# Second keys' attention scores: copied by ScalarE and masked by GpSimd in place of VectorE's masked multiply, in a newly ordered kernel

## The reference

```
x = x + tanh(g_xattn) * performer(layernorm(x), ctx, ctx)
x = x + tanh(g_ffn)   * ffn(layernorm(x))

performer:  q' = exp(proj_q) + 1e-4,  k' = exp(h_k + proj_k - max h_k) + 1e-4
            out[t] = sum_{s<=t} (q'[t].k'[s]) v[s] / sum_{s<=t} (q'[t].k'[s])
ffn:        h = rms(x); q = h Wq; k,v = (h Wdown) Wup
            att = softmax over heads of q.k;  x = x + (att v) Wo
            h2 = rms(x);  x + sum_e gate_e(h2) * (h2 We[e])
```

## Time and profile before

| | |
|---|---|
| median of 3 runs | 1069.57 us |
| the profiled execution's own time | 1069.42 us |
| span of its core | 1067.6 us, 32201 instructions |
| PE | 1012.6 us busy (95%), 12870 matmuls |
| DVE | 961.4 us busy (90%) |
| ACT | 758.7 us busy (71%) |
| POOL | 752.5 us busy (70%) |
| granted TensorE clock | 0.997 of full speed on average |
| chain that ended last | PE 87%, DVE 5%, POOL 4% |

### The profile page before, as it was taken

One profiled execution on the slowest core, in us unless ns is written; L12 is line 12 of the kernel. 1 busy time (PEld: TensorE's weight loads), 2 busy tenths in 40 slices (PEclk: granted clock), 3 DMA queues, 4 the chain that ended last, 5 costly groups with the idle time before them and its releaser, 6 DMA issues.

```text
span 1067.6 us, 32201 instructions
## 1 busy us (share of the span) xinstructions
PE 1012.6 (95%) x12870; PEld 831.4 (78%) x12870; DVE 961.4 (90%) x2176; ACT 758.7 (71%) x1564; POOL 752.5 (70%) x1111
## 2 busy tenths in 40 slices
PE   1568999999999999999999999999999999999998
PEld 0447788788888888888888888888888888888787
DVE  7778888999999999999999999999999999998996
ACT  6678877776677777668777666877766687776541
POOL 4578877787677778767778766777876677787531
PEclk9989999999999999999999999999999999999999
DMA  9501000011000001100100100010111000000000
GB/s 311 169 21 31 12 24 29 31 31 31 23 28 25 22 31 31 32 21 24 29 22 32 32 31 22 21 32 21 32 32 31 22 22 31 22 21 12 12 11 30
DMA packets 38915, 38.67 MB, mean 36 GB/s; under 512 B 3440, under 2 KB 38512, under 8 KB 38768
## 3 DMA queue, kind: packets, MB, share of 16 engines
q1 hardware_dynamic: 38384, 36.59, 10.9%
q0 software_dynamic: 384, 0.04, 0.0%
HBM read 28.23 MB, written 8.39 MB: 34 GB/s over the span
## 4 chain that ended last, share of the span: by engine, by line
PE 87%; DVE 5%; POOL 4%; issue 1%; ACT 1%; DMA 0%; SPq 0%; POOLq 0%; DVEq 0%; ACTq 0%
PE ps L2302 15%; PE ps L2304 14%; PE ps L2303 14%; PE ps L2333 10%; PE ps L2348 9%; PE ps L2341 5%; PE ps L2317 5%; PE ps L2382 3%; PE ps L2373 3%; PE ps L2296 2%; PE ps L2358 2%; DVE hk L1770 2%; PE ps L2366 1%; PE ps L2367 1%; PE ps L2325 1%
## 5 line engine op out<-in xcount | busy, mean ns | idle before, releaser
L1434 DVE SCALAR_TENSOR_TENSOR z<-ps,gate,z 128x256 f32<-128x256 f32 x512 | 238.5, 472 | 37.9 <-PE ps L2304 29.0
L2302 PE MATMUL ps<-we_hi,h_hi 128*128 128x512 f32 (+2 forms) x640 | 240.5, 376 | 0.6 <-DVE z L1434 0.4
L2304 PE MATMUL ps<-we_hi,h_lo 128*128 128x512 f32 (+2 forms) x640 | 224.1, 350 | 0.0
L2303 PE MATMUL ps<-we_lo,h_hi 128*128 128x512 f32 (+2 forms) x640 | 223.7, 349 | 0.0
L2302 PEld LDWEIGHTS ps<-we_hi,h_hi 128*128 128x128 f32 x640 | 120.4, 188 | 36.7 <-issue 12.6
L2333 PE MATMUL ps<-qf,kf 64*128 64x256 f32 x1024 | 129.2, 391 | 9.1 <-POOL kf L549 4.5
L2304 PEld LDWEIGHTS ps<-we_hi,h_lo 128*128 128x128 f32 x640 | 120.2, 188 | 17.1
L2303 PEld LDWEIGHTS ps<-we_lo,h_hi 128*128 128x128 f32 x640 | 120.8, 189 | 11.5
L2333 PEld LDWEIGHTS ps<-qf,kf 64*128 64x128 f32 x1024 | 96.4, 191 | 29.8 <-issue 11.3
L2348 PE MATMUL ps<-att,v 128*32 128x256 f32 (+1 forms) x2048 | 109.0, 329 | 3.1 <-POOL att L540 0.9
L911 ACT ACTIVATE att<-ps 128x512 f32<-128x512 f32 x32 | 19.1, 597 | 116.8 <-PE ps L2333 116.7
(11 more groups left out here) (232 smaller groups left out, 3079.7 us busy)
## 6 DMA issues: line engine op xcount, KB each, us to landing
x_in<-in_x SPq DMA_DIRECT2D x32, 256.0 KB, 2.6
c_in<-in_ctx SPq DMA_DIRECT2D x32, 256.0 KB, 2.6
out<-z SPq DMA_DIRECT2D x32, 256.0 KB, 2.2
c_chunk<-in_ctx SPq DMA_DIRECT2D x14, 512.0 KB, 8.0
stage<-in_L_ffn_We SPq DMA_DIRECT2D x2, 1024.0 KB, 10.0
c_chunk<-in_ctx SPq DMA_DIRECT2D x2, 256.0 KB, 6.5
stage_b<-in_L_ffn_bup SPq DMA_DIRECT2D x1, 256.0 KB, 6.9
stage_q<-in_L_ffn_Wq SPq DMA_DIRECT2D x1, 256.0 KB, 6.4
```

The lines of the kernel that those rows point to most:

```text
L1434: return dve.scalar_tensor_tensor(out=z[b % 2][:, t, :], in0=ps[:, bank, offset:offset + D], scalar=gate[:, t, ex:ex + 1], in1=z[b % 2][:, ...
L2302: pe.matmul(out, a_hi(c), b_hi(c), start=(c == 0), stop=False)
L2303: pe.matmul(out, a_hi(c), b_lo(c), start=False, stop=False)
L2304: last = pe.matmul(out, a_lo(c), b_hi(c), start=False, stop=(c == C - 1))
```

## The change

The four steps `y00` to `y11` move from VectorE to ScalarE. There they are plain copies, without the mask:

```diff
-                dve.wait_ge(*at("Y0", b))
-                dve.tensor_tensor(att[:, 0, :, 2 * P:3 * P], ps[:, BANK["y00"], :].rearrange("p (j l) -> p j l", j=4),
-                                  causal[:, :].unsqueeze(1).to_broadcast([P, 4, P]), ALU.mult).then_inc(*up("y00", b))
+                act.wait_ge(*at("Y0", b))
+                act.activation(att[:, 0, :, 2 * P:3 * P], ps[:, BANK["y00"], :].rearrange("p (j l) -> p j l", j=4), ACT.Copy).then_inc(*up("y00", b))
...
-                pool.affine_select(out=att[:, 0, :, 0:P], in_=att[:, 0, :, 0:P], compare_op=ALU.is_ge, fill=0.0, base=0,
-                                   pattern=[[0, 4], [1, P]], channel_multiplier=-1).then_inc(*up("m00", b))
+                for own in (slice(0, P), slice(2 * P, 3 * P)):
+                    last = pool.affine_select(out=att[:, 0, :, own], in_=att[:, 0, :, own], compare_op=ALU.is_ge, fill=0.0, base=0,
+                                              pattern=[[0, 4], [1, P]], channel_multiplier=-1)
+                last.then_inc(*up("m00", b))
```

All orders, banks and semaphores are new. The steps `dn`, `qq`, `kv0`, `kv1` now stand in the slot for batch `n` (before, all but `qq` for `n - 1`), the loop runs from 5 to 29 (before, 6 to 30), 25 slots in both. Banks and waits that matter:

```diff
-BANK = dict(stab=0, fk0=6, fk1=4, fk2=3, fk3=7, fq0=0, fq1=2, fq2=4, fq3=1, x000=3, x001=1, x010=0, x011=5,
-            y00=3, y01=7, av0=3, x100=0, x101=2, x110=5, x111=4, y10=1, y11=6, av1=2, nd0=2, nd1=0, ht=1,
...
+BANK = dict(stab=2, fk0=5, fk1=2, fk2=4, fk3=3, fq0=5, fq1=2, fq2=3, fq3=7, x000=0, x001=6, x010=0, x011=1,
+            y00=4, y01=5, av0=3, x100=2, x101=0, x110=1, x111=5, y10=6, y11=2, av1=7, nd0=6, nd1=4, ht=3,
...
             def X10_(b):
+                if b >= 2:
+                    pe.wait_ge(*at("y11", b))
...
             def fkp_(b):
+                if b >= 1:
+                    pe.wait_ge(*at("y11", b - 1))
...
             def fq_(b):
-                if b in (1, 2):
-                    pe.wait_ge(*at("o_x", b - 1))
...
+                if b >= 2:
+                    pe.wait_ge(*at("d_lo", b - 2))
```

More of the change, by code:

```diff
@@ L194, in build @@
             signal("once_pe0", "first_turned first_all most_turned stab_all"),
[L195 to L207, removed]
+            signal("pe0", "fkp fk fq X00 Y1"),
+            signal("pe1", "Y0 av0 av1 av3 nt_t"),
+            signal("pe2", "X01 X11"),
+            signal("pe3", "X10"),
+            signal("pe4", "hn_t dn kv1 s"),
+            signal("pe5", "qq"),
+            signal("pe6", "kv0 pv"),
+            signal("pe7", "o_tr o h2_t1"),
+            signal("pe8", "h2_t0 mm0g mm00"),
+            signal("pe9", "mm1g mm01 mm02"),
+            signal("pe10", "mm10 mm11"),
+            signal("pe11", "mm12"),
+            signal("pe12", "mm13"),
+            signal("pe13", "mm03"),
+            signal("once_dve0", "zero_v1 sel_tok first_least first_most first less_first least_ least stabilizer kept less wq_lo wup_lo"),
             signal("keys_dve0", "key_sums"),
@@ L231, in build @@
[L231 to L241, removed]
@@ new lines, in build @@
+            signal("act4", "ek0 eq1 x000 x001 y10 x101"),
+            signal("act5", "ek3 eq0 y00 y11"),
+            signal("act6", "eq3 x010 nt0 nt1"),
+            signal("act7", "x011 x110 x111"),
+            signal("act8", "y01 x100"),
+            signal("act9", "hn ht_hi d_hi q_bd"),
+            signal("act10", "y p_bd ot_hi"),
+            signal("act11", "k_bd"),
+            signal("act12", "sq h2n h2_hi0 gexp"),
+            signal("act13", "h2_hi1"),
+            signal("once_pool0", "one_tri ident f_scale f_hi f_lo"),
@@ L387, in _ @@
             store_(1)
-            load_x_(7)
-            load_c_(8)
-            for n in range(6, NB + -1):
+            for n in range(5, NB + -2):
                 slot(n)
@@ new lines, in h2n_, with y10_ @@
+            @per_batch
+            def h2n_(b):
+                act.wait_ge(*at("r2", b))
+                for t in range(T):
+                    last = act.activation(h2n[:, t, :], y2[:, t, :], ACT.Copy, scale=r2[:, t:t + 1])
+                last.then_inc(*up("h2n", b))
+            @per_batch
+            def y10_(b):
+                if b == 1:
+                    act.wait_ge(*at("Y1", b))
+                act.wait_ge(*at("av0", b))
+                act.activation(att[:, 0, :, 2 * P:3 * P], ps[:, BANK["y10"], :].rearrange("p (j l) -> p j l", j=4), ACT.Copy).then_inc(*up("y10", b))
@@ L1055, in square_ @@
+                last.then_inc(*up("y", b))
             def square_(b):
```

3002 lines of the change are left out of this document (1497 added, 1505 removed).

## The result

The changed kernel takes 1085.24 us (median of 4, 1082.6 to 1085.54) against 1069.61 (1068.63 to 1070.08) for the kernel before on the same chip: a ratio of 1.0142, 95% interval 1.013 to 1.0154. It is slower by 15.6 us. The forecast was +5.4 us with a range up to 1083, so the direction was right and the size was not.

A forecast was written before the change was run, and what follows sets the result against it. The prediction took PE, busy for 95% of the span, to bound the kernel. 1069.42 us + 2.5 (spacing) + 3.0 (fill) + 0 (tail, new waits) made 1074.9, about 1075 with the 0.15 to the median; range 1066 to 1083.

The forecast's parts named there:

- Term 1: Spacing of PE's matmuls in the loop: the new slot is 0.1 us longer, +2.5 us over 25 slots, bounds 0 and +7.5.
- Term 2: The fill, PE's waits in the early batches: chains to features and scores change, sum +3.0 us, bounds -3 and +9.
- The wait before the scores of batch 3: In the fill: only four product rows stand between fq and the scores, so PE idles 3.7 us: +3.7.
- The gain at fq: In the fill: fq of batch 1 no longer waits 1.98 us for o_x, whose banks it needed: -2.0 us.
- Four copies more, 2.4 us: In the fill, batch 1 to 2: four more copies come before fkp and av3 can go: +2.4 us.
- -1.1: In the fill: 0.95 us before the scores of batch 2 and like pieces, counted as replaced by the new waits.
- 17 to 18 us of idle time: Sign for the fill's sum: PE idle that long between the first scores and 134 us.
- Term 3: Tail and start: the same chains and cover as before, 0 us; bound 2 us either way in the tail.
- the new waits: In the loop, X10 for y11 and fq for ek3 and d_lo: both fit, 0 us, bound +7.5.
- A: Rival: faster, DVE's shorter list gives back 5 us of PE's idle time in the fill, 1064.5 us; chance 0.20.
- B: Rival: one of the loop's two tight places misses, a wait of 0.3 us every slot, 7.5 more, 1082.5; chance 0.20.
- C: Rival: no change, fq's gain and DVE's shorter list cancel the chain, slot as long as before, 1070 us; chance 0.15.

The follow-up runs named there:

- h6: The changed kernel with 40, 24 and 32 matmuls that nothing reads ahead of X01(1), X00(2) and Y0(3), where TensorE idled: 1080.85 us.
- h5: The kernel before with 18 matmuls that nothing reads ahead of fq(1) and 40 ahead of X00(1), where TensorE idled: 1069.37 us.
- n2: The changed kernel with score copies cut to one column, second selects left out, and 40, 24 and 32 unread matmuls in three idle times: 1075.80 us.
- n1: The changed kernel with the moved work left out from batch 1 on: copies of one column, one select per mask: 1082.68 us.
- s1: The changed kernel with pv moved ahead of mm03 in the slot, which adds two changes of the array's division: 1103.4 us.
- b1: The kernel before with fk moved directly behind fkp, which takes away one change of the array's division per slot: 1067.2 us.
- n3: The changed kernel with only the second selects left out, copies kept, and 40, 24 and 32 unread matmuls in three idle times: 1078.57 us.

## Why the prediction was wrong in size

**Sum.** By the two traces, 15.7 us arise so. Up to X00 of batch 7 it is 10.6, with 12 matmuls left undone, which are 2.8 us (12 x 0.23): 13.4 for the same work. Of these, idle time is 8.0 (22.7 against 14.7) and half clock 4.6 (6.4 against 1.8 lost, an estimate). The 0.8 that are left fit five more changes of the array's division in the new fill, counted in the code, which would be some 1 us (not shown by a run). The loop adds 2.8 up to X00 of batch 31 (977.62 before, 991.09 now), less than its two waits alone, and the tail 2.2, which is those 12 matmuls less 0.6.

The experiments price two causes of this: the clock 4.4 (h6 against the changed kernel; 4.1 if the 0.3 that the kernel before gains in h5 is taken off) and the moved work 5.0 (h6 against n2), of which 1.5 is X10's wait in the slots. What is left of the idle time, some 5 us by n1's 19.9 against 14.8, belongs to the new order of the fill: that is read from the waits, and no run that moved steps of the fill gained anything. The parts are differences of separate kernels and overlap, as the clock falls behind idle time.

**Term 1, spacing +2.5: the size came out by luck.** The slot grew by 0.12 us and the time by 3.0, but two waits of 0.12 and 0.07 us, which had no term, are in it: 0.19 of a growth of 0.12. The -0.07 that is left is the spacing together with waits of the same kind that the kernel before has at places of its own (its weight loads wait in each slot, named as for POOL's `att`, for DVE's `h_lo` and for ACT's `att`), and the rows don't part these. So +2.5 us for the spacing is not shown. That a change costs some 0.2 us was right: s1 priced it at 0.17, b1 at 0.20 where it happens and 0.09 on the whole slot.

**Term 2, the fill +3.0: the step that failed.** For the same work it was 13.4 by X00 of batch 7, and 8.8 without the half clock, three times the +3.0 and just inside the bound of +9. The wait before the scores of batch 3 held (3.93 for +3.7). The gain at fq was 1.0 and not 2.0. "Four copies more, 2.4 us" as the whole price of the moved work was too small. It went by ACT's copies alone and gave POOL's second selects no term; n3 gives 2.3 us for the selects and 2.8 for the copies, the slots' share included. The "-1.1" for pieces replaced had no ground: batch 2 got 3.15 where 0.95 was, and 1.89 before dn(0). Its text said that 17 to 18 us of idle time would prove the sum; it is 22.1.

**The clock: missing.** The prediction counted idle microseconds at their own length. Two of its own rows showed 0.93 and 0.92 on either side of a 4.14 us wait; asked of the new waits, they would have warned that half clock comes with such a wait. It had no term and was worth 4.4 us.

**Term 3 and the new waits.** Their 0 failed, though not by much each. The layout had y11 end 0.2 us before X10 is due and d_lo with about as much before fq; X10 waits 0.07 us and fq 0.12, in every slot, together 25 x 0.19 = 4.7 us, within the bound of 7.5. The tail was bounded by 2 us; from X00 of batch 31 to the last matmul it grew from 86.0 to 88.8, with 2.8 us more of PE's busy time left at that point (86.65 and 83.89 us): the work that the new order of the fill had not done yet.

**Rivals.** A is out: DVE's 2.4 us a batch less gave nothing back, and it idled 12 us at the head of its line. B was right in kind: both of its tight places miss, by 0.19 us a slot in sum where it said 0.3, but the slot's distance of 31.34 hid it, being short of the 31.5 that B was to show. C is out.

**Range.** The high end was Rival B's 1082.5, a wait in every slot. The time got past it by another way: the fill came near its upper bound (8.8 of +9), and the clock, 4.6 more, had no term.

## What to carry to other kernels

An idle time at the start is worth more than its length: look for the granted clock in the microseconds behind it, before and after, and price new gaps with it. Work that moves to engines with room in the loop has no room in the fill; count it there batch by batch on every engine that gets some, and do not net it with guesses. A busy share near 100% does not show waits shorter than one instruction; compare the starts with a run in which the work waited for is left out. Count how often the array's division changes in the loop body: each is some 0.2 us a turn, and moving one small step next to its like gave the only gain here.
